# Retention and mixture-of-experts kernel: routing spread over three engines, group-norm moments ahead of `uT_l`, scatters redistributed over steps 2 to 6

## The reference, cut to what matters

```python
def block(h, p):                                   # four times, L0_attn
    r = _retention(h, wk)
    a, gate = jnp.split(r @ w1 + b1, 2, axis=-1)
    m = _groupnorm1(a * jax.nn.silu(gate) @ w2 + b2, gg, gb)
    y = m + h
    f = gelu(y @ wf1 + bf1_) @ wf2 + bf2_
    return _layernorm(f + y, lg, lb)

router_probs = softmax(x_flat @ gate_w)            # L0_ffn
expert_idx = argmax(router_probs, axis=-1)
expert_w = take_along_axis(router_probs, expert_idx[:, None], axis=1)[:, 0]
for e in range(NUM_EXPERTS):
    h = gelu(x_flat @ w1[e] + b1[e])
    y = h @ w2[e] + b2[e]
    out = out + where(expert_idx == e, expert_w, 0.0)[:, None] * y
```

## Time and profile before

| | |
|---|---|
| runs, us | 495.89, 495.62, 495.76; median 495.76 |
| profiled execution | 494.12 us; its span 492.4 us |
| PE, VectorE, ScalarE, GpSimd busy | 95%, 75%, 54%, 53% of the span |
| scatters in steps 2 to 6 | 6, 7, 7, 7, 5 |
| first and last scatter issued | 61.54 and 119.41 us |
| first expert tile on PE | 123.63 us |
| granted TensorE clock | 0.999, mean of the span |

### The profile page before, as it was taken

The page is one execution under the profiler, slowest core; times in us unless marked ns, Lnnn a source line. Parts: engine busy times, 40 slices in busy tenths (PEclk is TensorE's granted clock), DMA queues, the critical chain, the costliest instruction groups (busy, mean ns, idle before and its releaser), DMA issues.

```text
span 492.4 us, 9882 instructions
## 1 busy us (share of the span) xinstructions
PE 465.9 (95%) x3155; PEld 390.9 (79%) x3155; DVE 371.7 (75%) x1323; ACT 264.5 (54%) x557; POOL 258.6 (53%) x288
## 2 busy tenths in 40 slices
PE   6999789999999999999999999999999999999785
PEld 5787566766888898988898898898888888876554
DVE  4858878777786667786777777677768667877987
ACT  3922434444555466644446665455665545568564
POOL 4530088888535545445454544654454555555653
PEclk9999999999999999999999999999999999999999
DMA  9999811111521111111111111110111100062445
GB/s 264 243 135 178 338 33 38 40 40 31 113 82 44 60 61 63 42 60 39 33 67 59 62 40 63 40 68 27 66 49 50 45 33 7 11 176 24 43 43 87
DMA packets 47921, 36.89 MB, mean 75 GB/s; under 512 B 13352, under 2 KB 39280, under 8 KB 47840
## 3 DMA queue, kind: packets, MB, share of 16 engines
q1 hardware_dynamic: 41376, 28.93, 22.5%
q0 software_dynamic: 5968, 6.54, 6.2%
q10 hardware_dynamic: 528, 0.79, 0.5%
HBM read 16.27 MB, written 11.25 MB: 56 GB/s over the span
## 4 chain that ended last, share of the span: by engine, by line
PE 69%; POOL 10%; DVE 9%; issue 7%; DMA 2%; ACT 2%; SPq 0%; POOLq 0%; DVEq 0%
PE bank L1648 8%; PE bank L1547 7%; PE bank L1531 7%; POOL x_slots L510 5%; PE pair L1727 4%; PE pair L1736 4%; PE bank L1747 4%; PE pair L1693 4%; PE bank L1558 4%; PE bank L1559 4%; PE bank L1560 4%; PE pair L1738 3%; PE pair L1688 3%; PE bank L1614 2%; PE bank L1586 2%
## 5 line engine op out<-in xcount | busy, mean ns | idle before, releaser
L581 POOL TENSOR_TENSOR zhat<-zhat,all_lg 128x512 f32<-128x512 f32 x28 | 37.8, 1351 | 80.3 <-PE bank L1604 74.0
L1648 PE MATMUL bank<-all_f,G_sb 128*128 128x128 f32 x512 | 72.9, 275 | 0.0
L824 ACT ACTIVATE y_sb<-bank,gn_bi,gn_sc 128x512 f32<-128x512 f32 x30 | 23.4, 781 | 88.0 <-DVE gn_bi L1397 88.0
L1648 PEld LDWEIGHTS bank<-all_f,G_sb 128*128 128x128 f32 x512 | 67.3, 192 | 1.7 <-issue 1.7
L797 ACT ACTIVATE uT_h<-bank 128x512 fp32r<-128x512 f32 x30 | 17.9, 598 | 93.6 <-PE bank L1614 93.6
L465 POOL TENSOR_TENSOR ln_rs<-ln_ve,half_neg 128x4 f32<-128x4 f32 x31 | 32.5, 1048 | 34.9 <-DVE ln_ve L928 34.6
L1531 PEld LDWEIGHTS bank<-moe_w,h_T 128*128 128x128 f32 x312 | 39.5, 191 | 13.9 <-issue 13.9
L696 ACT ACTIVATE h_T<-bank,w_t 128x128 f32<-128x128 f32 x156 | 44.7, 374 | 4.8 <-PE bank L1547 4.8
L628 POOL DMA_INDIRECT y_rows<-yt,slot_info x39 | 40.9, 1049 | 11.1 <-POOL yt L625 11.1
L753 ACT ACTIVATE G_sb<-bank,all_par 128x512 f32<-128x512 f32 x62 | 41.6, 695 | 6.6 <-PE bank L1586 4.4
L1547 PE MATMUL bank<-xtT,w_t 128*128 128x128 f32 x312 | 43.0, 281 | 0.0
(11 more groups left out here) (222 smaller groups left out, 1248.7 us busy)
## 6 DMA issues: line engine op xcount, KB each, us to landing
w_t<-moe_w SPq DMA_DIRECT2D x39, 258.0 KB
x_slots<-moe_w SPq DMA_DIRECT2D x1, 2515.5 KB, 20.5
xt<-x_slots SPq DMA_DIRECT2D x39, 64.0 KB, 1.8
x_sb<-in_L_attn_x SPq DMA_DIRECT2D x8, 256.0 KB, 5.8
moe_w<-in_L_ffn_w SPq DMA_DIRECT2D x1, 2048.0 KB, 20.2
moe_w<-y_rows SPq DMA_DIRECT2D x8, 256.0 KB, 4.6
out<-in_L_attn_x SPq DMA_DIRECT2D x1, 1536.0 KB, 15.5
out<-moe_w POOLq DMA_DIRECT2D x6, 256.0 KB, 4.7
```

The costliest lines, as they stand in the source:

```text
L581: pool.tensor_tensor(zhat[:, b % 2, :, :], zhat[:, b % 2, :, :], all_lg[:, li, :].unsqueeze(1).broadcast_to([P, C, D]), ALU.mult)\
L1648: last = mm(dst, G_sb[:, k, at_c], all_f2[:, n // B, k, :], start=False, stop=k == 1)
```

## The change

Routing is divided anew. `shift_logits` becomes `top_logit` on VectorE (maximum and comparison straight from PSUM); ScalarE copies the logits to SBUF; GpSimd's `choose_expert` multiplies the mask by `iota_e` and makes the difference `r_c`. VectorE's `first_expert` takes the minimum and makes `r_oh`. ScalarE copies `total` to SBUF, VectorE keeps the scan, and GpSimd's `count_tokens` and `offsets` take over the small subtractions, the subtraction of `total`, the addition of the base and the product with `r_oh`. VectorE's `count_tiles` moves from the start of step 2 to step 1, ahead of `y_residual`; `add_rank` and `find_slots` stand around `gated` in step 2; `find_experts` moves from step 3 to step 2, behind `y_residual`. The zeroing of `r_prev` moves to the prologue. In step 1 VectorE now does `gn_moments` ahead of `split_u`, as in steps 2 to 6. The scatters are 9, 6, 6, 6 and 5. In steps 0 and 1 the routing instructions of GpSimd stand in `step`, so that in program order `choose_expert` comes ahead of the splits behind step 0.

```diff
+            pool.memset(r_prev[:, 0:1], 0.0).then_inc(r_zero, 1)
...
-            SCATTERS = {2: (0, 2, 4), 3: (2, 1, 4), 4: (2, 1, 4), 5: (2, 1, 4), 6: (2, 1, 2)}
+            SCATTERS = {2: (4, 2, 3), 3: (1, 2, 3), 4: (1, 2, 3), 5: (1, 2, 3), 6: (1, 2, 2)}
+            def choose_expert():
+                pool.wait_ge(ids_made, 4)
+                pool.wait_ge(r_top, 1)
+                pool.tensor_tensor(r_oh[:, :, :], r_oh[:, :, :], over_t(iota_e[:, :]), ALU.mult).then_inc(r_pick, 1)
+                pool.wait_ge(logits_out, 1)
+                pool.tensor_tensor(r_c[:, :, :], r_lg[:, :, :], over_e(r_mx[:, :]), ALU.subtract).then_inc(r_shift, 1)
+            def count_tokens():
+                pool.wait_ge(r_zero, 1)
+                pool.wait_ge(r_ran, 1)
+                pool.tensor_copy(r_prev[:, 1:E], r_cum[:, 0:E - 1, NT - 1]).then_inc(r_pool, 1)
+                pool.wait_ge(r_pool, 1)
+                pool.tensor_tensor(r_n[:, :], r_cum[:, :, NT - 1], r_prev[:, :], ALU.subtract).then_inc(r_counted, 1)
+                pool.wait_ge(r_shift, 1)
+                pool.tensor_tensor(r_lg[:, :, :], r_cum[:, :, :].rearrange("p e t -> p t e"),
+                                   r_tot[:, :, :].rearrange("p e t -> p t e"), ALU.subtract).then_inc(r_pool, 1)
+            def offsets():
+                pool.wait_ge(r_based, 1)
+                pool.wait_ge(r_pool, 2)
+                pool.tensor_tensor(r_lg[:, :, :], r_lg[:, :, :], over_t(r_base[:, :]), ALU.add).then_inc(r_offset, 1)
+                pool.wait_ge(r_ranked, 1)
+                pool.tensor_tensor(r_lg[:, :, :], r_lg[:, :, :], r_oh[:, :, :], ALU.mult).then_inc(r_own, 1)
...
                 tile_rows(l, t, EARLY)
+                if first and t == 0:
+                    choose_expert()
+                if first and t == 1:
+                    count_tokens()
                 scatter(l, t, 0)
...
                     gn_pow(s - 1)
+                if first and t == 1:
+                    offsets()
                 scatter(l, t, 1)
...
                     act.activation(r_a[:, :, :], r_c[:, :, :], ACT.Exp).then_inc(r_exp, 1)
+                    act.wait_ge(pe_prefix, 1)
+                    act.activation(r_tot[:, :, :], total.rearrange("p t e -> p e t"), ACT.Copy).then_inc(totals_out, 1)
...
                 u_high(s)
+                if first and t == 0:
+                    act.wait_ge(r_top, 1)
+                    act.activation(r_lg[:, :, :].rearrange("p t e -> p (t e)"), bank[7][:, 0:TE], ACT.Copy)\
+                        .then_inc(logits_out, 1)
...
+            def top_logit():
+                dve.wait_ge(pe_gate, B)
+                dve.wait_ge(ids_made, 4)
+                logit = bank[7][:, 0:TE].rearrange("p (t e) -> p t e", e=E)
+                chain(dve.tensor_reduce(r_mx[:, :], logit, AX, ALU.max))
+                dve.tensor_tensor(r_oh[:, :, :], logit, over_e(r_mx[:, :]), ALU.is_equal).then_inc(r_top, 1)
+            def first_expert():
+                dve.wait_ge(r_pick, 1)
+                chain(dve.tensor_reduce(r_ix[:, :], r_oh[:, :, :], AX, ALU.min))
                 dve.tensor_tensor(r_oh[:, :, :], over_t(iota_e[:, :]), over_e(r_ix[:, :]), ALU.is_equal)\
-                    .then_inc(r_shift, 1)
+                    .then_inc(chosen, 1)
...
+            def running_count():
+                dve.wait_ge(totals_out, 1)
+                dve.tensor_tensor_scan(r_cum[:, :, :].rearrange("p e t -> p (e t)"), ones[:, 0:TE],
+                                       r_tot[:, :, :].rearrange("p e t -> p (e t)"), 0.0, ALU.mult, ALU.add)\
+                    .then_inc(r_ran, 1)
...
             def count_tiles():
+                dve.wait_ge(r_counted, 1)
...
+            def add_rank():
+                dve.wait_ge(r_offset, 1)
+                dve.tensor_tensor(r_lg[:, :, :], r_lg[:, :, :], prefix, ALU.add).then_inc(r_ranked, 1)
             def find_slots():
-                chain(dve.tensor_tensor(r_lg[:, :, :], r_cum[:, :, :].rearrange("p e t -> p t e"), total, ALU.subtract))
-                chain(dve.tensor_tensor(r_lg[:, :, :], r_lg[:, :, :], prefix, ALU.add))
-                chain(dve.tensor_tensor(r_lg[:, :, :], r_lg[:, :, :], over_t(r_base[:, :]), ALU.add))
-                chain(dve.tensor_tensor(r_lg[:, :, :], r_lg[:, :, :], r_oh[:, :, :], ALU.mult))
+                dve.wait_ge(r_own, 1)
                 chain(dve.tensor_reduce(posf[:, :], r_lg[:, :, :], AX, ALU.add))
...
                 if first and t == 1:
-                    choose_expert()
-                if first and t == 2:
-                    count_tiles()
+                    first_expert()
                 mask(s)
                 if s:
                     gate_tanh(s - 1)
+                if first and t == 2:
+                    add_rank()
...
                 if s:
                     gated(s - 1)
                 if first and t == 1:
                     expert_weight()
+                    running_count()
+                if first and t == 2:
+                    find_slots()
...
                 if first and t == 0:
-                    shift_logits()
+                    top_logit()
                 if first and t == 1:
                     gelu_bias()
-                    count_tokens()
-                if first and t == 2:
-                    find_slots()
-                if first and t == 3:
-                    find_experts()
...
-                for stage in (gn_moments, split_u) if first and 2 <= t < B - 1 else (split_u, gn_moments):
+                for stage in (gn_moments, split_u) if first and 1 <= t < B - 1 else (split_u, gn_moments):
...
                 tile_in(l, t, LATE)
+                if first and t == 1:
+                    count_tiles()
                 y_residual(l, t)
+                if first and t == 2:
+                    find_experts()
...
                 if first and t == 1:
-                    pe.wait_ge(r_shift, 2)
+                    pe.wait_ge(chosen, 1)
...
                     pe.wait_ge(rows_done, 1)
+                    pe.wait_ge(logits_out, 1)
```

36 lines of the change are left out of this document (12 added, 24 removed).

## The result

The kernel with the change takes 491.55 us (median of 6 executions, 490.10 to 494.05), the one before 495.88 in the same comparison (6 executions). The ratio is 0.9918, with a 95% interval of 0.9897 to 0.9939: faster by 4.3 us. The forecast was 490.8, with a range of 489.5 to 493.0. The profiled execution took 491.49 us with a span of 489.3; against the one of before (494.12 and 492.4) that is 2.6 and 3.1 us. So the two profiles show less of a gain than the medians do, and why is one of the things to be found.

The account below looks back on a forecast made before the run. PE is busy 465.9 of 492.4 us, so time lies in its waits in steps 1 to 7. Gains of 3.2 up to M3 and 3 x 0.6 give 5.0: 495.76 - 5.0 = 490.8 us, range 489.5 to 493.0.

Parts of the forecast that it names:

- The course of steps 0 to 6: New timeline up to the start of step 6's means matmul, each moved instruction carried through the waits: 5.0 us gained.
- first f1: PE's first f1 matmuls in step 2: start at 49.15 us instead of 50.11, 0.96 gained.
- M2: Start of PE's group-norm means matmul that ends step 2: 55.8 us instead of 57.84.
- M3: Start of PE's group-norm means matmul that ends step 3: 70.0 us, gain 3.2.
- the cycle: One PE step in steps 4 to 6: 12.5 to 12.65 us against 13.20, 0.55 to 0.7 gained three times.
- M6: Start of PE's group-norm means matmul that ends step 6: gain 3.2 + 3 x 0.6 = 5.0 us.
- near miss of 0.02: Steps 4 to 6: GpSimd's htok ends at M+11.76, VectorE's gs instruction wants its turn at M+11.78.
- The costs taken from near rows: GpSimd durations borrowed from similar rows: 0.73 us per 128x256 broadcast operation, 1.27 per scatter with issue, first 0.25 longer.
- Collisions replace waits: Rival: GpSimd's work holds VectorE in step 1 and htok may still meet gs; gain 2.7 to 3.0, about 492.9; chance 0.17.
- Scatters stall behind the loads: Rival: scatters from 53.5 us stall while DMA engines are full; slower by 1.3, 497.1 us; chance 0.06.
- The early gain is covered: Rival: GpSimd operations near 2.5 us delay slots, 493.0, chance 0.08; at over 4 us each, 495.8, chance 0.04.
- the gain stays to the end: From step 7's first expert tile PE is nearly always busy in the same order, keeping 4.8 to 5.2 us.

Follow-up runs that it names:

- Experiment 6: The changed kernel with ten one-column memsets added on VectorE in the prologue, giving the old instruction count: 492.14 us, ratio 0.9936.
- experiment 3: The changed kernel with the scatter distribution of the kernel before (6, 7, 7, 7, 5): 494.36 us, ratio 0.9968.
- experiment 4: The changed kernel with split_u ahead of gn_moments again in step 1: 493.30 us, ratio 0.9952.
- experiment 9: The kernel before with idle matmuls (5 and 4) in PE's two long waits of the ending: 494.59 us, ratio 0.9962.
- experiment 2: The changed kernel with the scan moved from ahead of normalise_u to behind group_sums in step 1: 491.91 us, ratio 0.993.

## Why the prediction was right, and where it was not

**The course of steps 0 to 6 held.** Experiment 6 shows it at full clock, with the forecast in brackets (`pos` is the slots; gains are against the kernel before): first f1 49.21 (49.15), outputs 51.03 (51.04), `pos` done 53.01 (53.15), M2 55.68 (55.8), gate of step 3 57.86 (57.95), f1 61.11 (61.3), transposes 64.81 (64.7), M3 70.17 (70.0), the cycle 12.44 (12.5 to 12.65), M6 5.34 ahead of before (5.0), first tile 118.28 (118.5 to 119). The largest miss is 0.3. What made this possible is that each step was carried through the waits of its engine and not added up as busy time: VectorE lost 6.2 us of work and GpSimd gained 5.3, and neither number appears in the gain. Part of it was narrow: that `htok` ends within 0.01 us of the start of `gs` was in the forecast as a near miss of 0.02, and no row could tell it which way that would go. That it went well is luck, with 0.31 us of room behind it.

**The costs taken from near rows held.** 0.73 us for a 128x256 broadcast operation, 1.27 for a scatter with its issue whether or not the DMA engines are full, some 0.3 more for the first. Outside are one scatter of 1.36, the last ahead of `ln_rs` in step 2, and the strided subtraction, 1.06, which nothing waits for.

**What carried the gain.** The forecast gave 3.2 to the steps up to M3 and 1.8 to the three cycles up to M6. Experiment 6 has 3.05 (73.22 - 70.17) and 2.3. By experiment 3 the second part needs the new distribution: with the old one the cycle stays at 13.2. Over all the distribution is worth 1.35 at M6, since it costs 0.9 up to M3. Moments ahead in step 1 are worth 0.45 (experiment 4). For the rest, the slots being known at 53 instead of 60, only the timelines speak; it was not undone alone.

**The rivals.** Collisions replace waits (0.17): they are there, 0.79 and 0.82 on VectorE and 1.06 for one split, and covered; the near miss of `htok` and `gs` went well, 0.16 us. Experiment 3 shows what it costs when they meet. Scatters stall behind the loads (0.06): refuted by 0.96 to 0.98 us each at 56.38 to 58.93. The early gain is covered (0.08 and 0.04): refuted by 0.73 for GpSimd's operations.

**The step that failed** is "From there PE has its work in the same order and is nearly always busy, so that the gain stays to the end". At equal clock (experiment 6 against the kernel before) the change is 5.34 us ahead at M6, 5.32 at M7 and 4.67 at M29 (439.72 against 444.39), for 0.6 goes back in two steps whose tile matmuls start late, and 0.45 more outside the span. That leaves 4.2. The two kernels' executions at a mean clock of 0.999 and 1.000 agree: 494.12 before, 490.10 after, 4.0. So the forecast of 5.0 was 0.3 too low for the part that it worked out and 1.1 too high for the part that it took for granted, and came out 0.75 us low. What starts the tile matmuls late in those steps, and what lengthens the time outside the span, stays open.

**What was missing altogether** is the clock. One fall costs some 1.3 to 1.7 us: 1.5 at M3 for the one at 45 us, and for the first in the ending the stretch between two means matmuls goes from 11.65 us to between 12.9 and 13.3. The medians of both kernels contain falls, before in the ending, after there and at 45 us, and it is chance that they weigh about the same: 4.3 by the medians, 3.9 to 4.3 with the ending cleared, 4.0 without falls. The two profiles alone show 2.6, since the one of before has no fall and the one after has one. The forecast set its sum against the profiled execution of before (494.12) and then took it off the median, 1.64 higher, without asking what the 1.64 were. By experiment 9, 1.5 of them are falls of the clock.

## What to carry to other kernels

Where engines wait for each other in turn, carry each moved instruction through the waits; sums of busy time told nothing here. A small instruction that is held beside another engine's long one, and for which PE waits, can be worth a redistribution of its own: 0.7 us a step here. And before timing edits of half a microsecond look at the granted clock in 1 us stretches of several profiles: where a fall follows a wait of PE in some of them, as after the 2.6 us here, filling the waits with idle matmuls can both save time (1.5 us here) and shrink the spread (2.1 to 0.6 us), so that the edits can be told apart. And compare profiles at an early mark before believing a median: experiment 2 looked 0.4 us worse by the median and was 0.95 us better at M3, experiment 3 looked 2.8 worse and was 1.35 worse at M6.

## What was not expected of the hardware

- The clock can halve for some 3.4 us in one execution and not in another of the same kernel: the changed kernel has one at a mean of 1.000 beside the profiled one with the fall. At M1 = 44.98 with the same wait of 0.55 to 0.56 us it fell in that profile and held in the one of experiment 6. After waits of 2.6 us in the ending it fell in one profile of the kernel before (with thirteen idle semaphores) and held in the other.
- With idle matmuls in the waits of the ending no profile of four fell there, without them eight of ten did; idle matmuls in the short wait at 44 us did not stop the fall behind it.
- VectorE shows gaps of 0.25 to 0.34 us at "issue" ahead of `yt` whose place moved when ten instructions were added; the other nine profiles with the change have it at the same place as the changed kernel (212.87 to 215.72, 0.24 or 0.25), the other two without it at that of before (0.34 at 182.96 and 183.08). Of the four in the profiles of before, after and experiment 6 two were harmless (before at 182.73, experiment 6 at 426.46) and two stand in a step that is 0.35 us longer.
- The time outside the span is 1.70 to 1.83 us in all kernels without the change and 2.14 to 2.26 in all with it, and thirteen more semaphores don't make the difference.
- Indirect scatters are issued at nearly the same rate with the DMA engines full and idle: 0.96 to 0.98 us and 0.3 between at 56.38 to 58.93, while they moved up to 492 GB/s, and a median of 1.02 over all 32; the longest, 1.36, came at 67 GB/s.
